# A diffusion block chain on one core: layer 0 in row products with batch 0 first, and the modulation of three layers beside the QR columns

## The reference

```
U, _ = qr(P)                                  # P is 288 x 64
v = silu(cond) @ W.T + b                      # 2016 values for each batch
A = skew-symmetric 64 x 64 matrix of v
R = expm(A)
z = x @ U
x = x + (z @ R - z) @ U.T
```

```
six = split(silu(cond) @ W_ada + b_ada, 6)
h = layernorm(x) * (1 + six[1]) + six[0]
x = x + six[2] * attention(h)
h = layernorm(x) * (1 + six[4]) + six[3]
x = x + six[5] * mlp(h)
```

## Time and profile before

| | |
|---|---|
| median of 3 runs | 2091.69 us |
| range of the 3 runs | 2080.91 to 2091.76 us |
| profiled execution, its own time | 2106.0 us |
| profiled execution, span from first to last instruction | 2104.2 us |
| mean granted clock of TensorE (1 is 2.4 GHz) | 0.911 |
| busy share of the span: PE, DVE, ACT, POOL | 90%, 59%, 44%, 26% |

### The profile page before, as it was taken

The page is one execution under the profiler, slowest core; times in us unless marked ns, Lnnn a source line. Parts: engine busy times, 40 slices in busy tenths (PEclk is TensorE's granted clock), DMA queues, the critical chain, the costliest instruction groups (busy, mean ns, idle before and its releaser), DMA issues.

```text
span 2104.2 us, 29869 instructions
## 1 busy us (share of the span) xinstructions
PE 1904.2 (90%) x10842; PEld 1298.8 (62%) x10842; DVE 1233.4 (59%) x2748; ACT 924.5 (44%) x1582; POOL 547.0 (26%) x541
## 2 busy tenths in 40 slices
PE   7899858999989878999978998999989889999998
PEld 6687534444438766444435876444438778888997
DVE  6755526777735456777742655777734655546554
ACT  0200023766664434777654533767573432222221
POOL 1111131222245533333233533222141220101000
PEclk9965567999989988999987999999989999999999
DMA  7000013333210021232220021332300010001000
GB/s 236 1 1 1 8 46 93 95 101 90 93 34 10 1 80 58 86 97 79 79 73 20 4 80 50 96 106 87 104 26 35 20 31 16 26 23 34 1 23 23
DMA packets 68985, 114.08 MB, mean 54 GB/s; under 512 B 14586, under 2 KB 29498, under 8 KB 68840
## 3 DMA queue, kind: packets, MB, share of 16 engines
q1 hardware_dynamic: 68840, 112.18, 17.6%
HBM read 80.95 MB, written 30.70 MB: 53 GB/s over the span
## 4 chain that ended last, share of the span: by engine, by line
PE 72%; ACT 10%; DVE 9%; issue 4%; DMA 2%; POOL 2%; SPq 1%; ACTq 0%; DVEq 0%; POOLq 0%
PE ps L1550 23%; PE ps L1632 13%; PE ps L1601 8%; PE ps L1587 7%; PE ps L1678 5%; PE ps L1572 4%; ACT Pr L1373 3%; PE ps L1497 2%; PE ps L1653 2%; PE ps L1453 2%; ACT xn L1272 1%; DVE negmax L996 1%; ACT HQ L1348 1%; PE ps L1476 1%; PE ps L1477 1%
## 5 line engine op out<-in xcount | busy, mean ns | idle before, releaser
L996 DVE TENSOR_REDUCE negmax<-ps 128x1 f32<-128x512 f32 x768 | 490.1, 683 | 185.1 <-PE ps L1572 179.4
L1373 ACT ACTIVATE Pr<-ps 128x512 f32<-128x512 f32 x768 | 406.8, 601 | 155.1 <-PE ps L1587 153.6
L1384 ACT ACTIVATE g<-ps,b1col 128x512 f32<-128x512 f32 x216 | 148.5, 687 | 451.9 <-PE ps L1550 439.1
L1180 DVE CAST G<-g 128x512 fp32r<-128x512 f32 x216 | 125.9, 583 | 323.8 <-ACT g L1384 322.9
L1587 PE MATMUL ps<-QK 55*128 55x512 f32 x768 | 249.3, 515 | 53.9 <-ACT Pr L1373 51.6
L1632 PE MATMUL ps<-W2a,G 128*128 128x288 f32 x1728 | 269.7, 307 | 2.0 <-DVE G L1182 2.0
L1632 PEld LDWEIGHTS ps<-W2a,G 128*128 128x128 f32 x1728 | 251.8, 196 | 14.8 <-DVE G L1182 4.2
L1587 PEld LDWEIGHTS ps<-QK 55*128 55x128 f32 x768 | 98.4, 194 | 242.6 <-ACT Pr L1373 142.8
L1572 PE MATMUL ps<-QK 54*128 54x512 f32 x768 | 202.8, 437 | 29.2 <-DVE negmax L996 17.1
L1601 PE MATMUL ps<-Pr,V 128*32 128x512 f32 x1536 | 222.0, 652 | 0.0
L1182 DVE TENSOR_TENSOR G<-g,G 128x512 fp32r<-128x512 f32 x216 | 167.0, 773 | 7.4
(11 more groups left out here) (205 smaller groups left out, 2652.7 us busy)
## 6 DMA issues: line engine op xcount, KB each, us to landing
QK<-heads_t SPq DMA_DIRECT2D x192, 144.0 KB
heads_t<-stage SPq DMA_DIRECT2D x96, 252.0 KB
QK<-heads_t SPq DMA_DIRECT2D x192, 72.0 KB
raw<-in_w SPq DMA_DIRECT2D x18, 432.0 KB
raw<-in_w SPq DMA_DIRECT2D x12, 576.0 KB
WA<-in_ada_w SPq DMA_DIRECT2D x3, 1728.0 KB, 15.5
heads_t<-stage SPq DMA_DIRECT2D x24, 144.0 KB
QK<-W1a SPq DMA_DIRECT2D x192, 2.0 KB, 2.4
```

The source lines that it names most:

```text
L996: dve.tensor_reduce(negmax[:, m % 2, t, h:h + 1], ps[:, a_bank(s, i), :], AX, ALU.max, negate=True).then_inc(a_free, 1)
L1180: dve.tensor_copy(G[:, n % 3, 0, :], g32[:, n % 2, :]).then_inc(g_hi, 1)
L1373: act.activation(Pr[:, t % 2, 2 * half + pair, :], ps[:, (16 * s + u) % 3, :], ACT.Exp, scale=SCALE).then_inc(b_free, 1)
L1384: act.activation(g32[:, n % 2, :], ps[:, 4, :], ACT.Gelu if l == 1 else ACT.Gelu_apprx_tanh, bias=b1col[:, e, s % FT:s % FT + 1]).then_inc ...
```

## The change

The order of the loop over the columns is kept, but its parts are new.

- **The column on DVE.** The updates touch only the live part of a row (65 columns of `GI`, and 63 - j columns of `T`). The copy of the row and the `NB` operation leave DVE. A second matmul spreads the same row of `GI` into another bank, ACT copies it (`gram_copy`), POOL takes both the root and the inverse root (`root_pair`), and ACT scales the row with it (`gram_scale`). DVE does `reduce_gram(j)` and then `reduce_top(j - 2)`, so that this path has one column more.
- **The skew matrix.** It is computed in four row products (512 streaming columns each, the four conditions stationary), in slots 4, 7, 10 and 13. The rows go through DRAM back into `Up`, and DVE masks them in slot 20.
- **exp.** A round is one entry (every second column from 23 to 59) without the product with the identity; POOL adds the identity beforehand (`add_unit`, two additions of 64x256 a round).
- **The modulation.** 18 row products of 288 streaming columns, 12 of them turned into columns by small matmuls (`turn_columns`). The biases are a further row of the weights. They stand in slots 41 to 64. The splits of the first three weight pieces on POOL move into slots 29, 33 and 47, and their first halves on ACT into 28, 32 and 46.
- **The end of layer 0.** `ym` and `l0` become items of the second part; batch 0 comes first and its statistics follow at once, and the other three batches lie between the steps of batch 0. The opening has 34 ticks in place of 27, and the first step's query scores use five banks in place of two.
- **Start.** The pads that DVE set to zero are gone except two, and two small loads stand no longer ahead of those that the start waits for.

```diff
-PTICKS = 27
+PTICKS = 34
...
 def opening():
...
-    out += [(4 + c, "ln1", 0, 0, c) for c in range(3)]
...
+    for b, (t, u) in enumerate(((0, 1), (2, 3), (6, 7), (9, 10))):
+        out += [(t, "ym", 0, b, 0), (u, "l0", 0, b, 0)]
+    out += [(1, "stats1", 0, 0, t) for t in range(TT)] + [(1, "mean1", 0, 0, 0)]
+    out += [(t, "ln1", 0, 0, c) for c, t in enumerate((5, 7, 9))]
...
+            def add_unit(r):
+
+                unit = (ident[0:D, 0:D] if r < DEGREE - 1 else ident2[:, :]).unsqueeze(1).broadcast_to([D, B, D])
+                for x in range(2):
+                    pool.wait_ge(exp_ev, 2 * r + x + 1)
+                    pool.tensor_tensor(EM[:, r % 2, x], EX[:, r % 2, x], unit, ALU.add).then_inc(exp_add, 1)
...
+            def root_pair(j):
+
+                pool.wait_ge(g_copied, j + 1)
+                pool.tensor_tensor(roots[:, j, :], RG[:, j % 2, j:j + 1].broadcast_to([D, 2]), halves[:, :], ALU.pow).then_inc(root_ready, 1)
...
             def reduce_gram(j):
...
-                dve.scalar_tensor_tensor(out=GI[:, :], in0=row, scalar=m, in1=GI[:, :],
+                dve.wait_ge(bc_r, j + 1)
+                dve.scalar_tensor_tensor(out=GI[:, live], in0=row[:, live], scalar=m, in1=GI[:, live],
                                          op0=ALU.mult, op1=ALU.add).then_inc(gi_upd, 1)
-                dve.tensor_copy(RG[:, k, :], row[:, 0:D]).then_inc(n2_ready, 1)
...
             def reduce_top(j):
...
+                dve.wait_ge(g_scaled, j + 1)
+                dve.tensor_scalar(den, sh, roots[:, j, 0:1], alpha, ALU.mult, ALU.add).then_inc(dve_done, 1)
                 dve.wait_ge(dve_done, step())
                 dve.reciprocal(rd, den).then_inc(dve_done, 1)
+                ready = step()
+                dve.scalar_tensor_tensor(out=W[:, live], in0=RG2[:, j % 2, live], scalar=sh, in1=row[:, live],
+                                         op0=ALU.mult, op1=ALU.add).then_inc(dve_done, 1)
+                step()
+                dve.wait_ge(dve_done, ready)
+                dve.scalar_tensor_tensor(out=m, in0=T[:, j:j + 1], scalar=rd, in1=below[:, j:j + 1],
+                                         op0=ALU.mult, op1=ALU.mult).then_inc(dve_done, 1)
                 dve.wait_ge(dve_done, step())
...
+                dve.scalar_tensor_tensor(out=T[:, live], in0=W[:, live], scalar=m, in1=T[:, live],
                                          op0=ALU.mult, op1=ALU.add).then_inc(t_upd, 1)
...
+            for j in range(D + 2):
+                if j < D:
+                    reduce_gram(j)
+                if j >= 2:
+                    reduce_top(j - 2)
...
+            def gram_copy(j):
+
+                act.wait_ge(bc_r, j + 1)
...
+                act.activation(RG[:, j % 2, j:D], ps[0:D, 2 + j % 2, j:D], ACT.Copy, scale=4.0).then_inc(g_copied, 1)
...
+            def gram_scale(j):
+
+                act.wait_ge(root_ready, j + 1)
...
+                act.activation(RG2[:, j % 2, j + 1:D], RG[:, j % 2, j + 1:D], ACT.Copy, scale=roots[:, j, 1:2]).then_inc(g_scaled, 1)
...
+            def skew_rows(n):
...
+                for c, rows in enumerate((128, 128, 33)):
+                    ins = mm(ps[0:B, 6 + n % 2, :], csil[0:rows, c, :], Wsk[0:rows, c, N * n:N * n + N], start=c == 0, stop=c == 2)
+                ins.then_inc(skew_mm, 1)
...
+            def row_product(l, v, bank):
...
+                for c, rows in enumerate((128, 128, 34)):
+                    ins = mm(ps[0:B, bank, 0:C], csil[0:rows, c, :], WA[l][0:rows, c, C * v:C * v + C], start=c == 0, stop=c == 2)
+                ins.then_inc(arow_mm, 1)
...
+            def turn_columns(l, v, bank):
+                n = AROW["arow", l, v, 0]
+                pe.wait_ge(arow_ev, n + 1)
...
 BACKGROUND = sorted(
...
+    [(4 + 3 * n, "skew", n) for n in range(4)] + [(20, "turn")] + [(23 + 2 * r, "exp", r) for r in range(ROUNDS)] +
+    [(t, "x", n // 3, n % 3) for n, t in enumerate((15, 16, 17, 19, 21, 22, 26, 28, 30, 34, 36, 38))] +
+    [(t, "y", b) for b, t in enumerate((18, 24, 32, 40))] +
+    [(t, "high", n) for n, t in enumerate((28, 32, 46))] + [(t, "split", n) for n, t in enumerate((29, 33, 47))] +
...
+    [(41 + 4 * n // 5, kind, l, v, 5) for n, (kind, l, v) in enumerate(
```

More of the change, by code:

```diff
@@ L38 @@
 PLACED = 16 * 8
-PTICKS = 27
+SKP = 2048
+PTICKS = 34
 def ticks():
@@ L739, in low_weights @@
                 pool.wait_ge(raw_lo, n + 1)
-            for n in range(3):
-                low_weights(n)
+            for j in range(D):
+                root_pair(j)
+                for slot, kind, *args in BACKGROUND:
+                    if kind == "split" and slot == j:
+                        low_weights(*args)
+                    if kind == "turn" and slot + 2 == j:
+                        add_unit(0)
+                    if kind == "exp" and slot == j and args[0] < ROUNDS - 1:
+                        add_unit(args[0] + 1)
+            pool.tensor_tensor(rootd[:, :], roots[:, :, 0], ident[0:D, 0:D], ALU.mult).then_inc(diag_ready, 1)
+            pool.wait_ge(diag_ready, 1)
             phase_end(pool)
@@ L1244, in _ @@
+            for j in range(D + 1):
+                if j < D:
+                    gram_copy(j)
+                if 1 <= j < D:
+                    gram_scale(j - 1)
+                for slot, kind, *args in BACKGROUND:
+                    if kind in background and slot + (2 if kind == "turn" else 0) == (j if j < D else max(j, slot)):
+                        background[kind](*args)
             act.wait_ge(mid_mm, 1)
@@ L1461, in skew_transpose, with exp_round @@
                 ins.then_inc(skew_t, 1)
[L1463 removed]
+            def exp_round(r):
                 if r == 0:
[L1466 to L1478 removed]
@@ L1480, in ada_products @@
-            def ada_products(l, piece):
-                if piece == 0:
+                    pe.wait_ge(skew_done, 2)
+                for x in range(2):
+                    pe.wait_ge(exp_ev, 2 * r + 2)
+                    pe.wait_ge(exp_add, 2 * r + x + 1)
+                    for b in range(B):
+                        left = BB[:, 1 - x, b, :] if r < DEGREE - 1 else EX[:, r % 2, 1 - x, b, :]
+                        ins = mm(ps[0:D, 6 + x, D * b:D * b + D], left, EM[:, r % 2, x, b, :], start=True, stop=True)
+                    ins.then_inc(exp_mm, 1)
@@ L1509, in _ @@
+            background = dict(x=x_transpose, y=y_product, skew=skew_rows, turn=lambda: skew_transpose(), exp=exp_round,
+                              arow=row_product, acol=turn_columns)
             spread_gram(0)
-            for j in range(D):
+            spread_top(0)
+            for j in range(D + 1):
                 if j + 1 < D:
                     spread_gram(j + 1)
-                for at, kind, *args in BACKGROUND:
-                    if at == j:
+                for slot, kind, *args in BACKGROUND:
+                    if kind in background and slot == (j if j < D else max(j, slot)):
```

565 lines of the change are left out of this document (279 added, 286 removed).

## The result

The changed kernel took 2068.0 us (median of 5 runs, 2065.3 to 2076.7) where the kernel before took 2087.1 us beside it (5 runs, 2080.9 to 2091.8): ratio 0.991, 95% interval 0.988 to 0.994. It is 19 us faster; I had said 69, and 2023 us. The profiled execution of after took 2076.7 us, 29 less than that of before (2106.0).

What follows compares the result with a forecast made beforehand. DVE and PE in turn were taken to set the column loop's pace. Loop -59, start -1, loop end to `ym` -3, normalisation -9, `ln1` to QKV +2.7: -69 from 2091.7 gives 2023 us; own range 2008 to 2040.

Steps and rivals of the forecast that it cites:

- the modulation at +28 us: Loop, 23 modulation columns: PE near the high clock level adds 28 us beyond DVE's 41.
- the 1.2 GHz case: Rival: the modulation runs at 1.2 GHz and adds 71 us in place of 28, total 2065 us; chance 0.13.
- The prices of both levels: Modulation: four columns take 10.7 us at the high clock level or 19.5 us at the low one.
- the clock stays up: Rival: wide streaming keeps PE's clock high in the loop, 31 us less than forecast, about 1992 us; chance 0.24.
- DVE's column of 1.8 us: Loop: DVE's work per column falls from 2.38 to 1.8 us, 115 us for 64 columns if nothing else sets the pace.
- Columns 0 to 14 with the skew: Start of the loop: predicted 41 us, with the four skew columns near the low clock level adding 14 us.
- the slow rival: Rival: the new root path sets each loop column, mean 3.95 us, total 2157 us; chance 0.02.
- the 12.5 in the list of signs: Behind the loop: first transposes of `ln1` expected some 12.5 us behind `ym`.
- POOL's locks, +9,: Loop: POOL's additions and splits hold up DVE operations reading two SBUF tiles, adding 9 us.
- the 11 us that I had reckoned for this: Loop: by the skill's rule, POOL's root would hold up DVE in 41 columns, 11 us more; left out of the forecast.
- Last reciprocal to `ym`: End of the loop: 12.6 us before, predicted 3 less, with a last row product replacing DVE's waits.
- the rival with the high clock: Rival: PE's clock stays high, skew 5.5, y 5.5, exp 0, modulation 20, POOL 4, about 1992 us; chance 0.24.

Runs made afterwards that it cites:

- the filled run: Kernel after with the exponential's operands and the third product of skew rows and row products on 128 partitions, results exact: 2020.9 us, ratio 0.970 to the kernel before.
- the run with wide operands: Kernel after with the stationary condition operand of skew rows and row products widened from 4 to 128 columns with zeros: 2077.7 us, ratio 0.995 to the kernel before.
- the padded tail: Kernel after with the operands of the exponential, `ym` and `l0` zero-padded to 128 partitions: 2040.5 us, ratio 0.977 to the kernel before.
- the filled kernel before: Kernel before with the third products of skew and modulation on 128 partitions by repeating the first channels (wrong results): 2062.6 us, ratio 0.989 to the kernel before.

## Why the prediction was wrong, step by step

**The step that failed: the modulation at +28 us**, that is "so I lie near the high level". It measured 98.3 us in 22 columns, 59 over DVE's 39.6, where my low price was 71 in 23 columns. That is 30 of the 37 us by which the loop is longer than I said (98.3 for 68). I had priced the 1.2 GHz case at 2065 us and gave it 0.13; that 2068.0 lies within 3 us of it is in part luck, since the modulation cost 59 us and not that case's 71, and other terms more (below). The prices of both levels are about right: four columns took 18.8 us for 19.5 at the low one, and with the third product filled the stretch takes 61.8 us, 22 over the floor, against 20 at the high one. What I misjudged was the granted clock. The argument was that 288 columns an instruction would keep it up, as the 512 of L1441 seemed to the earlier trace rows. I never asked how many partitions these instructions cover. The rows of the kernel after by shape, loop only, show it (count, busy us, mean ns):

```profile
L1585 PE MATMUL ps<-WA,csil 128*4 128x288 f32 x68 | 33.5, 642 | 0.0
...
L1585 PE MATMUL ps<-WA,csil 34*4 34x288 f32 x34 | 18.1, 631 | 0.0
```

A third of the products run on 34 partitions and take as long as the others, and filling these partitions alone gave back 45 us. PE's busy share tells nothing of it: 122.9 of 130 us (95%) at 0.54 here, 54.7 of 60 (91%) at 1.00 in the filled run. The Trainium skill (TensorE: Matmul & The Clock Gate, Part 1) describes the clock as following how busy the array has been; by that rule the padding changes nothing (2068 us), and these runs disagree with it unless busy means more than these rows count. The change itself did three things to the clock: it took the zeros from the exponential (15 us by the medians, 23 up to the first QKV product, measured by putting them back), took them from `ym` and `l0` (3 us or less up to that product), and kept a short third product in every row, in a stretch that is nearly all PE's. The kernel before has short third products too, of 32 to 34 partitions; filling them there gave 25 us.

**A reading that was wrong from the start: the clock of 1.00 in the earlier trace rows.** I took the first 58 us of before as fast. The spread of `T`, the same instruction all along, says otherwise (kernel before, PE in order of time):

```profile
60.32 0.48 PE L1423 MATMUL ps<-T,ident 128*64 128x64 f32 x2 [0.26 <-DVE T L910]
...
67.21 0.32 PE L1476 MATMUL ps<-EF,BB 128*64 128x64 f32 x2
...
68.35 0.33 PE L1423 MATMUL ps<-T,ident 128*64 128x64 f32 x2
```

It took 0.42 to 0.48 us in every column up to 67 us, with a clock of 1.00 in the row, and 0.33 from there to 113: the 1.2 GHz level ended only in the second half round of the exponential, with operands on 128 partitions. Without the zero padding, with the same instructions in the same order, the same spread stays at the long duration until past 87 us (that run, PE in order of time), and the granted clock of this stretch, 0.95, is the same in both:

```profile
87.52 0.47 PE L1423 MATMUL ps<-T,ident 128*64 128x64 f32 x2 [0.34 <-DVE T L910]
...
95.42 0.33 PE L1423 MATMUL ps<-T,ident 128*64 128x64 f32 x2
```

In the run with wide operands the reading is off in the same way. Its stretch from 24 to 30 us:

```profile
24.00:30.00 6.00, 6.00 (x10) 2.13 (x10) 1.56 (x8) 0.00 (x0) 0.00 (x0) 1.00 1.02 278
```

The kernel after has 0.50 there, and the spreads take 0.46 us in both. The Trainium skill (TensorE: Matmul & The Clock Gate, Part 1) warns that traced clock events have been seen to be unreliable on trn2; these rows agree. Had I read durations, "the clock stays up" (0.24) would have had less.

**Right:** DVE's column of 1.8 us (1.79 to 1.83 wherever nothing stands beside it). The first reciprocal 2.1 us earlier (I said 1 of start). Columns 0 to 14 with the skew: 44.0 for 41 us, the low level as I had taken it. DVE's denominator (L979) never waited for the root's path; it stood idle once, for 0.3 us, and behind DVE's own operation, so the slow rival (2157) fell. The mask never waited. From `ym` to the first transposes 14.2 us (the terms of the sum give 13.1; the 12.5 in the list of signs doesn't follow from them). Behind the first QKV product 1810.0 us where before had 1813.6.

**POOL's locks, +9,** were of the right size: 8 DVE operations that read SBUF tiles were drawn out by 6.5 us in all in the kernel after, and 22 by 11.7 in the filled run (those above 0.3 us, each counted above an ordinary 0.25). Each of the 8 lies beside an addition or a split. The sums are upper bounds of what they cost, since some lie in columns that PE sets. One of the filled run's beside a split, POOL and DVE in order of time:

```profile
101.36 2.00 POOL L822 TENSOR_TENSOR WQ<-raw,WQ 128x864 fp32r<-128x864 f32 x1
...
101.44 1.93 DVE L975 SCALAR_TENSOR_TENSOR small<-GI,small,below 64x1 f32<-64x1 f32 x1
```

The root didn't lock: the DVE operation at 11.04 us above has two inputs in SBUF, lies inside POOL's root (10.89 to 11.58) and takes its usual 0.21 us. With a root in every column, DVE's columns still take 1.79 to 1.83 us, so the 11 us that I had reckoned for this are nil.

**Mis-sized terms beside it.** Last reciprocal to `ym` 12.4 us for 9.6, and `ln1` to the first QKV product 15.9 for 12.1: both at 1.2 GHz. The filled run has 7.8 for the first; the padded tail 11.6 for the second. A skew row took up to 5.37 us for 4.9. I had priced `l0` at 2.2 us, from operands with zeros in 64 of their 128 partitions, though the change makes them 64. The terms of the rival with the high clock add up to 29.5 us and not 31, which changes nothing.

The sum of the misses in the profiled execution: loop 36.9, `ln1` to the first QKV product 3.8, the last reciprocal to `ym` 2.8, `ym` to `ln1` 1.1, the start 1.1 less and what follows 3.6 less: 39.9 us, which is 2076.7 - 2037 to the rounding. The gain missed by 50 us (69 forecast, 19 measured); the other 10 are the executions': the profiled one of before lies 18.9 us above its median of 5, that of after 8.7, and I had put 14.3 under both.

**Open:** why the filled kernel before stays at 0.67 from 118 to 248 us (4 streamed columns, or its weight loads); whether the partitions of the stationary or of the streaming operand count, since every padding widened both; why the clock stays low with no short product in a row and one full product fewer (0.56); what lies between 34 or 64 and 128 partitions; and why columns 0 to 14, the same instructions, took 41.4 us in one run with repeated channels and 35.0 in the other (three of the four skew columns took 3.5 us in the one with 35.0; in the other they took 4.8 to 6.3).

## What to carry to other kernels

Before pricing a matmul at the fast clock, read its shape in partitions as well as its columns: in a contraction cut as 128 + 128 + 34 the short product took as long as a full one (631 and 642 ns), and here filling it lifted the clock of a whole stretch (118 to 178 us) from 0.59 to 1.00. A version that drops it and a full one stayed at 0.56. The filling was worth 45 us, or 54 with the exponential's padding, where the whole change had been worth 19. A change that removes "useless" padding on an engine that is the bound should be priced with the padding's clock taken away. Check the level of the clock by the duration of one instruction that recurs, not by the granted clock alone.

## What the runs showed of the hardware that was not expected

- TensorE's clock followed the partitions covered by operands, zeros included. With 34 partitions made 128 in the third product of skew rows and row products, the six instructions of a row went from 3.13 to 1.62 us and the kernel from 2068.0 to 2022.7 us; with 128 made 64 in before, it went from 2087.6 to 2126.3. 128 stationary columns for 4 brought nothing (2077.7), nor 128 partitions for 4 in the turning products (2017.6), nor dropping the short and one full product of each row (granted clock 0.56).
- The granted clock reads 1.00 in the first 58 us of before, while spreads take 0.47 us that take 0.33 later, and it doesn't change when the padding is taken away and the long spreads last some 20 us longer.
- POOL's `pow` of 64x2 (0.69 us) didn't hold up DVE's operations of two SBUF inputs (0.21 us inside it, as usual); its additions of 64x256 and splits of 128x864 did (0.76 us and 1.93 us for the same 0.21).
